# Output product of an attention layer from rounded parts, and a value product without its wholly masked blocks

## The reference

```python
x = x + attn(layernorm(x))            # x: 4 batches x 512 rows x 256
x = x + moe(layernorm(x))             # 8 experts, 2 per row, capacity 640, hidden width 1024

# attn: 32 query heads in 8 groups of 4 that share a key head and a value head; head width 64
q, k, v = split(x @ W_qkv); q, k = rope(q), rope(k)
mask = (q_pos >= k_pos) & (q_pos < k_pos + 64)
attn = where(mask, -inf, q @ k.T / 8)              # 512 x 512 for each head
w = softmax(concat(attn, sink))[..., :-1]
out = (w @ v) @ W_out                              # W_out: (32 * 64) x 256
```

## Time and profile before

| | |
|---|---|
| median of 3 runs | 1071.03 us (1070.24 to 1071.81) |
| span of the profiled execution, first to last instruction | 1063.8 us |
| period of a group inside the attention part, one example | 23.54 us |
| PE busy | 97% |
| DVE busy | 86% |
| ACT, POOL busy | 61%, 62% |

### The profile page before, as it was taken

How to read it: one execution, slowest core, us unless ns; L and a number is a source line. 1 busy time by engine, 2 the same in 40 slices (tenths; PEclk the granted TensorE clock), 3 DMA queues, 4 the chain that set the end, 5 groups by cost and what they waited for, 6 DMA issues and landing times.

```text
span 1063.8 us, 32339 instructions
## 1 busy us (share of the span) xinstructions
PE 1032.3 (97%) x13013; PEld 729.8 (69%) x13013; DVE 918.9 (86%) x1962; ACT 653.7 (61%) x1670; POOL 663.4 (62%) x607
## 2 busy tenths in 40 slices
PE   6899999999999999999999999999998999999996
PEld 4466666666666666666666666666566999999995
DVE  6999999999999999999999999999966777677773
ACT  4676667666667666667776656777654455544451
POOL 5657776767666888666777877667762422233332
PEclk8999999999999999999999999999999999999998
DMA  3544555544333344333343344333324344454421
GB/s 94 150 114 117 129 135 130 137 118 131 95 84 81 95 110 105 97 100 79 80 111 101 95 131 111 94 86 98 100 80 159 87 121 121 126 125 124 101 44 21
DMA packets 115574, 112.11 MB, mean 105 GB/s; under 512 B 35264, under 2 KB 103936, under 8 KB 115296
## 3 DMA queue, kind: packets, MB, share of 16 engines
q1 hardware_dynamic: 97648, 90.29, 31.3%
q0 software_dynamic: 7296, 8.55, 5.0%
q10 hardware_dynamic: 10480, 11.20, 3.8%
HBM read 74.84 MB, written 21.83 MB: 91 GB/s over the span
## 4 chain that ended last, share of the span: by engine, by line
PE 60%; DVE 35%; issue 2%; ACT 1%; DMA 0%; SPq 0%; POOLq 0%; DVEq 0%
PE bank L1536 21%; DVE probs_ring L1124 15%; DVE probs_t L1133 13%; PE bank L1701 11%; PE bank L1512 11%; PE bank L1712 7%; DVE heads_sb L1153 4%; PE bank L1715 4%; PE bank L1568 1%; PE bank L1441 1%; PE bank L1676 1%; PE bank L1458 1%; PE bank L1476 1%; PE bank L1596 1%; DVE neg_max L1124 0%
## 5 line engine op out<-in xcount | busy, mean ns | idle before, releaser
L841 ACT ACTIVATE probs_ring<-probs_ring,neg_max 128x512 f32<-128x512 f32 x512 | 365.9, 717 | 210.2 <-DVE neg_max L1124 209.4
L1124 DVE CUSTOM_DVE_ANT_0 probs_ring<-bank,mask,sink_neg 128x512 f32<-128x512 f32 x512 | 360.3, 738 | 24.9 <-PE bank L1512 23.8
L1133 DVE STREAM_TRANSPOSE probs_t<-probs_ring 128x1024 f32<-128x1024 f32 x256 | 317.8, 1241 | 0.2 <-ACT probs_ring L841 0.2
L1512 PE MATMUL bank<-qk_st 64*128 64x512 f32 x1024 | 280.6, 624 | 11.6 <-DVE neg_max L1124 7.4
L1536 PE MATMUL bank<-probs_t,v_quads 32*64 32x256 f32 x8192 | 247.9, 381 | 0.0
L1536 PEld LDWEIGHTS bank<-probs_t,v_quads 32*64 32x64 f32 x8192 | 179.3, 132 | 75.4 <-issue 48.1
L670 POOL TENSOR_TENSOR chunk_sb<-chunk_sb,rope_sb 128x512 f32<-128x512 f32 (+1 forms) x94 | 119.8, 1275 | 111.1 <-issue 80.6
L789 POOL DMA_INDIRECT out<-expert_sb,slots x40 | 77.8, 1945 | 150.6 <-DVE expert_sb L1385 143.3
L1512 PEld LDWEIGHTS bank<-qk_st 64*128 64x128 f32 x1024 | 85.3, 185 | 77.0 <-DVE neg_max L1124 41.5
L1043 ACT ACTIVATE hidden<-bank,b_sb 128x320 f32<-128x320 f32 x128 | 60.5, 524 | 107.1 <-PE bank L1701 107.1
L675 POOL TENSOR_TENSOR qk_st<-chunk_sb,swap_sb 128x512 f32<-128x512 f32 (+1 forms) x94 | 120.0, 1276 | 7.4
(11 more groups left out here) (189 smaller groups left out, 1352.5 us busy)
## 6 DMA issues: line engine op xcount, KB each, us to landing
v_quads<-v_rows SPq DMA_DIRECT2D x128, 128.0 KB
recip_wide<-recip_rows SPq DMA_DIRECT2D x64, 256.0 KB
w_raw<-in_L_ffn_w SPq DMA_DIRECT2D x14, 1024.0 KB, 8.2
swap_sb<-chunk_sb SPq DMA_DIRECT2D x314, 32.0 KB
w_raw<-in_L_attn_W_qkv SPq DMA_DIRECT2D x32, 256.0 KB, 2.9
slots<-slot_rows SPq DMA_DIRECT2D x9, 662.5 KB, 4.0
slot_rows<-x2T ACTq DMA_DIRECT2D x8, 662.5 KB, 6.2
w_raw<-in_L_attn_W_qkv SPq DMA_DIRECT2D x64, 64.0 KB, 2.7
```

The lines of the kernel that those rows point to most:

```text
L841: nc.scalar.activation(probs[(g * UNITS + n) % RING][:, :], probs[(g * UNITS + n) % RING][:, :], ACT.Exp, bias=neg_max[j][:, n:n + 1], sca ...
L1124: nc.vector.tensor_tensor_reduce(probs[(g * UNITS + n) % RING][:, :], SCORE[SCORE_OF[n // 2][n % 2]][:, :], mask[:, L - P - t * P:2 * L - ...
L1133: nc.vector.transpose(probs_t[j][:, :, (h // 2) * (2 * P):(h // 2 + 1) * (2 * P)] .rearrange("p b (h q) -> p h b q", h=2)[:, :, :, t * BLK ...
L1512: nc.tensor.matmul(SCORE[SCORE_OF[n // 2][hh]][:, :], qk_st[j][half, h // 2, t * P:(t + 1) * P], qk_st[j][half, PAIRS, :], start=True, sto ...
```

## The change

The output product of all groups but the last becomes three products of rounded parts, on the whole array. ACT rounds `heads_sb` to `heads_hi` (two instructions a group), POOL subtracts to get `heads_lo` (two), and PE does 24 matmuls of 128 rows x 256 columns in place of 16 of 64 rows. The weights are split once for each of the 8 key heads (ACT `wo_high`, POOL `wo_low`, in the first batch), stored to memory (`keep_wo`), and read back for each group of the later batches (`load_wo_again`). `recip_wide` now shares its memory with `heads_lo`, so the spreading of the reciprocals waits for the output product of the group before. The steps move: the halves of the output product to 30 and 32, the copies to 31 and 33, the residual to 35, and the sum of the rotation of Q01 from -11 to -9. The value product leaves out the 32 x 32 blocks that the band hides: such a matmul covers 3 of 4 blocks of rows, and where the hidden one is an inner block, the matmul becomes two.

```diff
-        Y_AT = {28: 0, 30: 1}
-        Y_FIRST_OUT_AT, Y_OUT_AT, RESIDUAL_AT = 30, 31, 38
+        HEADS_HI_AT, HEADS_LO_AT = {26: 0, 27: 1}, {22: 0, 24: 1}
+        WO_HI_AT, WO_LO_AT = 18, 19
+        Y_AT, LAST_Y_AT = {30: 0, 32: 1}, {28: 0, 30: 1}
+        Y_FIRST_OUT_AT, Y_OUT_AT, RESIDUAL_AT = 31, 33, 35
+        ROT_SUM_AT = {2: Q23, -12: KV, -9: Q01}
...
+        recip_wide = heads_lo[:, :, :].bitcast(F32)
...
             def recip_spread(g):
                 sp.wait_ge(s_recip_out, g * 16 + 16)
                 if later(2 * g):
-                    sp.wait_ge(s_heads, 2 * g + 1)
+                    sp.wait_ge(s_y, 2 * g + 1)
...
+            def keep_wo(k):
+                sp.wait_ge(s_wo_lo, k + 1)
+                sp.dma_start(wo_store[k], wo_parts[k % 2]...).then_inc(s_wo_kept, 16)
+            def load_wo_again(g):
+                sp.wait_ge(s_wo_kept, (g - 1) * 16 if g < NKV + 2 else NKV * 16)
+                sp.wait_ge(s_y, 2 * (g - 2) + 2 + 1)
+                sp.dma_start(wo_parts[g % 2]..., wo_store[g % NKV]).then_inc(s_wo_back[g % 2], 16)
...
+            def heads_low(g, half):
+                pool.wait_ge(s_heads_hi, 2 * g + half + 1)
+                nc.gpsimd.tensor_tensor(heads_lo[:, banks_of, :], heads_sb[:, banks_of, :],
+                                        heads_hi[:, banks_of, :].bitcast(F32), ALU.subtract).then_inc(s_heads_lo, 1)
...
+            def heads_high(g, half):
+                act.wait_ge(s_heads, 2 * g + half + 1 + 1)
+                nc.scalar.activation(heads_hi[:, banks_of, :], heads_sb[:, banks_of, :], ACT.Copy).then_inc(s_heads_hi, 1)
...
                     nc.scalar.activation(y_sb[1][:, 1, :], PV[3][:, 0:D], ACT.Copy).then_inc(s_y_first_out, 1)
+                    nc.scalar.activation(y_sb[1][:, 0, :], PV[1][:, 0:D], ACT.Copy).then_inc(s_y_out, 1)
...
-                    for a in range(QUADS):
+                    for i, a in enumerate((0, 1, 2, 3) if g == GROUPS - 1 else (1, 3, 0, 2)):
...
+            PV_ORDER = [(c, turn) for c in (0, 1, 2, 3) for turn in (1, 0, 2, 3)]
+            def value_step(j, c, turn, first, last):
+                for a in range(QUADS):
+                    d = (a + turn) % QUADS
+                    rows = slice(a * BLK, (a + 1) * BLK)
+                    hidden_tile = TPB * d + c + 1 - TPB * a
+                    tiles = [t for t in range(TPB) if t != hidden_tile]
+                    runs = [tiles[:hidden_tile], tiles[hidden_tile:]] if 0 < hidden_tile < TPB - 1 else [tiles]
+                    for p in range(PAIRS):
+                        ...
+                        for run in runs:
+                            q = slice(run[0] * BLK, (run[-1] + 1) * BLK)
+                            ins = nc.tensor.matmul(out[:, :, q], v_quads[j][rows, d, c * HD:(c + 1) * HD], seen[:, :, q],
+                                                   start=first, stop=last)
...
+                    for a in (3 - half, 1 - half):
+                        for h in range(2):
+                            for i, (heads, wo) in enumerate([(heads_hi, wo_hi), (heads_hi, wo_lo), (heads_lo, wo_hi)]):
+                                ins = nc.tensor.matmul(PV[a][:, 0:D], heads[:, a, h * P:(h + 1) * P], wo[:, h, :],
+                                                       start=(h == 0 and i == 0), stop=(h == 1 and i == 2))
+                        ins.then_inc((s_y_high, s_y)[half], 1)
```

More of the change, by code:

```diff
@@ L557, in _ @@
                 swap_halves(g + 1, Q23)
+                if 0 < g <= NKV:
+                    keep_wo(g - 1)
+                if g >= NKV:
+                    load_wo_again(g)
                 if g % NKV == 1 and g > NKV:
@@ L676, in rotate, with wo_low @@
                                         ALU.add).then_inc(s_rot, 1)
+            def heads_low(g, half):
+                pool.wait_ge(s_heads_hi, 2 * g + half + 1)
+                banks_of = odd_or_even(half)
+                nc.gpsimd.tensor_tensor(heads_lo[:, banks_of, :], heads_sb[:, banks_of, :],
+                                        heads_hi[:, banks_of, :].bitcast(F32), ALU.subtract).then_inc(s_heads_lo, 1)
+            def wo_low(k):
+                pool.wait_ge(s_wo_hi, k + 1)
+                hi, lo = [wo_parts[k % 2][:, part, :, :] for part in range(2)]
+                nc.gpsimd.tensor_tensor(lo, wo_raw[k % 2][:, :, :], hi.bitcast(F32), ALU.subtract).then_inc(s_wo_lo, 1)
             pool.wait_ge(s_small_in, 16)
@@ L680, in pool_step @@
                 if n in ROT_AT and (g > 0 or ROT_AT[n] == Q23):
-                    c = ROT_AT[n]
-                    rotate(g, j, c)
+                    rotate_products(g, ROT_AT[n])
+                if n in ROT_SUM_AT and (g > 0 or ROT_SUM_AT[n] == Q23):
+                    rotate_sum(g, j, ROT_SUM_AT[n])
+                if n in HEADS_LO_AT and g < GROUPS - 1:
+                    heads_low(g, HEADS_LO_AT[n])
+                if n == WO_LO_AT and g < NKV:
+                    wo_low(g)
                 if n == (SECOND_SPLIT_AT if g == 1 else SPLIT_AT) and 0 < g < GROUPS - 1:
@@ L838, in act_step @@
                     v_copy(g)
+                if n in HEADS_HI_AT and g < GROUPS - 1:
+                    heads_high(g, HEADS_HI_AT[n])
+                if n == WO_HI_AT and g < NKV:
+                    wo_high(g)
                 if 0 <= n < UNITS:
@@ L1530, in pe_step @@
                             pe.wait_ge(s_chunk_out, (g + 2) * CHUNKS + KV + 1)
-                    for blk in PV_AT[n]:
-                        c, d = divmod(blk, TPB)
-                        for a in range(QUADS):
-                            rows = slice(a * BLK, (a + 1) * BLK)
-                            for p in range(PAIRS):
-                                ins = nc.tensor.matmul(PV[a][p * HD:(p + 1) * HD, 0:2 * P],
-                                                       v_quads[j][rows, d, c * HD:(c + 1) * HD],
-                                                       probs_t[j][rows, blk, p * 2 * P:(p + 1) * 2 * P],
-                                                       start=(blk == 0), stop=(blk == BLOCKS - 1))
-                    if blk == BLOCKS - 1:
+                    for i in PV_AT[n]:
+                        ins = value_step(j, *PV_ORDER[i], first=(i == 0), last=(i == BLOCKS - 1))
+                    if i == BLOCKS - 1:
                         ins.then_inc(s_pv, 1)
@@ new lines, in pe_step @@
+                    pe.wait_ge(s_heads_lo, 2 * g + half + 1)
+                    if half == 0:
+                        if g < NKV:
+                            pe.wait_ge(s_wo_lo, g + 1)
+                        else:
+                            pe.wait_ge(s_wo_back[j], ((g - NKV) // 2 + 1) * 16)
+                    wo_hi, wo_lo = [wo_parts[j][:, part, :, :] for part in range(2)]
+                    for a in (3 - half, 1 - half):
[4 more added lines that the diff above has]
+                        ins.then_inc((s_y_high, s_y)[half], 1)
@@ new lines, in pe_step @@
+                if n in LAST_Y_AT and g == GROUPS - 1:
+                    half = LAST_Y_AT[n]
+                    pe.wait_ge(s_heads, 2 * g + half + 1 + 1)
+                    for a in (2 * half, 2 * half + 1):
+                        for h in range(2):
+                            ins = nc.tensor.matmul(
+                                PV[half][:, (a % 2) * D:(a % 2 + 1) * D], heads_sb[:, a, h * P:(h + 1) * P],
+                                wo_raw[j][:, h, :], start=(h == 0), stop=(h == 1))
+                    ins.then_inc(s_y, 1)
```

75 lines of the change are left out of this document (39 added, 36 removed).

## The result

The changed kernel takes 1187.88 us (median of 4 runs, 1185.96 to 1192.59) against 1071.42 us (4 runs, 1070.24 to 1071.86) for the kernel before on the same chip: a ratio of 1.1098, 95% interval 1.1072 to 1.1124. The direction is the one predicted. The size is not: 1123 us was forecast, and 1187.88 lies outside the range of 1090 to 1176.

The account below looks back on a forecast made before the run. A chain alternating between DVE and PE was taken as the bound, not PE alone. Per period 1.83 + 0.15 - 0.2 = 1.78 us, times 29 = 52, giving span 1116 and time 1123 us; range 1090 to 1176.

Parts of the forecast that it names:

- It applies in periods 2 to 30: Summing step: where a pair, an output half and scores 2 meet, 1.78 us a period, 29 x 1.78 = 52.
- scores 4 later: PE's queue: scores 4 stand behind pair 0, half 1, scores 2 and pair 1, starting at 14.3 instead of 12.47, +1.83 us.
- The order of scores, halves and pairs: PE's queue each period: scores 12, scores 14, half 0, scores 0, pair 0, half 1, scores 2, pair 1, scores 4.
- With the semaphore I take +0.15: Value product behind scores 4 waits for the output copies, now behind the chunk's copy on ACT: 15.5 against 15.4, +0.15 us.
- I go near the lower end: -0.2: Value product itself, bounds -0.35 (columns left out) and +0.6 net (additional matmuls): taken as -0.2 us.
- the serial rival: Value product's split matmuls run one behind the other: +2.2 us a group, 70 more, about 1190; chance 0.06.
- Cover is 0.8 us; what POOL is later than that adds one for one: POOL's heads_lo: first ends at 4.8, before half 0 at 5.6; second at 7.4, before the sink's argument at 7.71.
- So it has the room: POOL's residual and wo_low fit before the KV rotation, which waits for a chunk copy itself 1.8 later: no cost.
- The clock rival: PE's idle stretches drop its clock to the lower level: 29 x 1.75 = 51 us more, 1174; chance 0.12.
- its sign: What would show the lower PE clock: a granted clock under 0.95 in the attention part.
- the forecast added 7.2: Last step of the sum: the runs' median stands 7.2 us above the span, so span 1116 gives 1123.
- the expected saving of the three products: Output product on PE: a half takes 1.65 us in place of 1.73, so each saves only 0.08.

Follow-up runs that it names:

- Run 9: Changed kernel with ACT's last two copies of the output one unit earlier, ahead of the chunk's copy: 1172.09 us, ratio 1.0933.
- Run 6: Kernel before with value matmuls shortened only where the hidden block is at an edge, none cut in two: 1063.87 us, ratio 0.9947.
- run 1: Kernel before with only the change's value product, hidden blocks left out and two of sixteen steps with split matmuls: 1078.56 us, ratio 1.0116.
- run 5: Changed kernel with the route's scatters on POOL issued six units later, past the sink's sum: 1182.11 us, ratio 1.105.
- Run 8: Run 7's kernel with no value matmul cut (only edge blocks left out) and the last scatters ahead of the last group's heads_lo: 1102.03 us, ratio 1.0303.
- run 7: Changed kernel with output halves and copies in their old slots and the heads' parts made earlier on ACT and POOL: 1109.08 us, ratio 1.0373.
- Run 10: Changed kernel with one of the three output products (coarse parts only), all parts still made: 1173.5 us, ratio 1.0974.
- run 12: Run 8's kernel with one of the three output products, the two small ones left out: 1111.05 us, ratio 1.0388.
- run 4: Changed kernel with both output halves and the output copies back in their old slots: 1136.98 us, ratio 1.0681.
- run 3: Changed kernel with the first copies of the output one unit earlier on ACT, ahead of the last exponential and the sink's: 1149.65 us, ratio 1.0796.

## Why the prediction was right in direction and wrong in size

Scores 4 came late by the mechanism that was forecast. What failed are the sizes of the terms of one period, the value product's with its sign, and the step "It applies in periods 2 to 30", which let one period without route work stand for all and put the route's ten periods and the last two at nothing more. I take the terms of the sum in the group that starts at 699.33, 26.55 us, against the same group of the kernel before, 23.56 (not the one of the earlier trace rows, whose successor holds route work in the changed kernel). Starts are those of each piece's first record.

| term | predicted | measured |
|---|---|---|
| scores 4 later | +1.83 | +2.17 (12.49 to 14.66) |
| value product waits for copies | +0.15 | +0.58 (1.06 to 1.64) |
| value product itself | -0.2 | +0.24 |
| sum a period | +1.78 | +2.99 (the quiet ones: +3.12 on average) |
| POOL behind the halves | 0 | 11.1 us in all, in seven periods |
| DVE beside POOL | 0 | 5.8 us in all, in three periods |
| the rest of the route's ten periods | 0 | 2.8 us in all |
| last two periods | 0 | +6.8 us |

**The order of scores, halves and pairs held, and nearly to the tenth.** Scores 14 at 4.62 (predicted 4.6), half 0 at 5.67 (5.6), scores 0 at 7.29 (7.2), pair 0 at 9.11 (9.0). The idle stretches are 1.05 by DVE and 0.69 by ACT's copy, and DVE waits 1.76 before unit 2. A half takes 711.65 - 710.03 = 1.62 (1.65). Of the 0.34 that are missing 0.1 is there when pair 0 starts, and the rest comes after: pair 0 took 1.59, priced at 1.40; scores 2 and pair 1 took 2.35, priced at 2.25. The 1.40 was read from a place where no full-array work followed, and now a half follows; that this is the reason was not tried. The mechanism was right, its size short.

**"With the semaphore I take +0.15" failed.** I added the chunk's copy and the two `y` copies up to 15.5 and set it against 15.4, but left out that the chunk's copy starts 0.23 after scores 4 do, and that the value matmul follows the copies by another 0.26. The wait was there, priced at a quarter of its size. Run 9 shows the whole term: taken away, it gives 0.65 a quiet period.

**"I go near the lower end: -0.2" failed in sign.** The lower bound was the columns saved, the upper one the cuts. Run 6 and run 1 split them: -0.18 and +0.40 a group. Each was inside its bound (-0.35 and +0.93). The choice between them was made with no row for it, and it was the wrong one. The rule by which the serial rival was priced, from the Trainium skill ("TensorE: Matmul & The Clock Gate", part 3, the mechanism), would have made the cuts cost 2.2. Run 1 does not bear that out; its cuts cost 0.40 a group.

**"Cover is 0.8 us; what POOL is later than that adds one for one" named the right path and was not followed up.** It prices POOL from one period, and the 0.8 is half 0's cover. The scatters stand behind the second `heads_lo`, and there the prediction's own times leave 7.71 - 7.4 = 0.3 (measured 0.48). Seven periods have two scatters in just that place: the sink's argument is 1.95 late, and PE idles 2.2 to 2.5 us before pair 0 in place of 0.69: 31.0 - 29 x 0.69 = 11 us. In three of the seven, those that end at groups 14, 22 and 29, the clock also fell, within 1.3 us of the end of that wait. The seven exceed the quiet 3.12 by 13.9 in all; the 2.8 beyond the waits lie in these three. Moving the scatters gave 10.2 back in the ten periods, and there the clock fell in none of them (run 5).

**"So it has the room" counted POOL's room and not DVE's beside it.** The other three periods, those that end at groups 12, 20 and 28, exceed 3.12 by 5.8 us in all (6.1 in run 5, with the scatters moved). In them DVE has small instructions of the route late in the period. In the kernel before they ran in POOL's idle time ahead of the KV rotation. Now DVE comes to them 2.5 to 4.2 us later, and the rotation starts at most 0.4 later, so the two run side by side. Changed kernel, DVE, then POOL, and the third of the DVE lines in the kernel before:

```profile
605.65 0.21 DVE L1385 TENSOR_REDUCE slot_f<-picked 128x8 f32<-128x64 f32 x1
605.90 0.43 DVE L1388 TENSOR_TENSOR full<-slot_f,slot_end 128x8 f32<-128x8 f32 x1
606.36 1.19 DVE L1389 SCALAR_TENSOR_TENSOR scatter_idx<-full,slot_f 128x8 uint32<-128x8 f32 x1
607.94 1.05 DVE L414 TENSOR_TENSOR xn<-gates,top_sum 128x32 f32<-128x32 f32 x1
```
```profile
605.03 1.27 POOL L702 TENSOR_TENSOR chunk_sb<-chunk_sb,rope_sb 64x512 f32<-64x512 f32 x1 [1.76 <-issue]
606.27 1.26 POOL L703 TENSOR_TENSOR swap_sb<-swap_sb,rope_sb 64x512 f32<-64x512 f32 x1
607.60 1.26 POOL L713 TENSOR_TENSOR qk_st<-chunk_sb,swap_sb 64x512 f32<-64x512 f32 x1
```
```profile
535.43 0.17 DVE L1315 SCALAR_TENSOR_TENSOR scatter_idx<-full,slot_f 128x8 uint32<-128x8 f32 x1
```

The last three DVE instructions end 0.03, 0.02 and 0.13 us after POOL's L702, L703 and L713. In the whole attention part nine DVE instructions are lengthened like this, from 0.16 to 0.19 us each to between 0.30 and 2.64, by 8.6 us together: 4.4, 2.1 and 2.0 in just these three periods. In the kernel before none is. No run moved them by themselves, so that they are the periods' excess is read from the trace and not tried.

**The last two periods were not looked at.** The last scatters feed a chain (scatter, gather, turning on PE) that the last value product waits for, and both `heads_lo` of group 30 came ahead of them. Run 8, with the scatters in front, has 19.69 where run 7 has 25.79.

**The clock was not the cause, nor innocent.** Inside the attention part the clock fell five times against once before. At 1.75 each the four additional falls are at most 7 of the 117 us. The clock rival (one in each period) is refuted: the granted clock is 0.988, and its sign was one under 0.95. In runs 10 and 12, where PE has less to do between its waits, the clock spends more time at the lower level (48 us against 17, and 27 against 7).

**Does it add up?** 29 x 3.12 = 90.5, scatters 11.1, DVE beside POOL 5.8, the rest of the ten periods 2.8, the last two periods 6.8: 117.0. The forecast had 51.6 of it. What it lacked is 29 x (3.12 - 1.78) = 38.9 in terms that it had and sized too small, 19.7 in the route's ten periods and 6.8 in the last two, both put at nothing. From there to the runs' medians the forecast added 7.2; the median stands 3.9 above the new span.

**Where the expected saving of the three products went.** Run 10 answers it from the other end. Even with two thirds of them gone the kernel is 1.0974. The length of the output product is paid once a period, in half 1's place; what costs is that its operands need a step on ACT and one on POOL between `heads_sb` and PE. In late slots (the changed kernel) that pushes scores 2; in early ones (runs 4, 7, 8) PE waits for POOL. Of the 0.110, the slot of one copy gives 0.030, all slots back 0.042, and earlier parts 0.031 more. (The first and the second overlap: run 4 moves the copy too. The runs were made in different batches, and each figure is a difference of two ratios, good to about 0.005.) After run 8, 0.030 stay. In it POOL has no gap between the parts and PE still waits 0.34; the rest of its 0.69 a period I did not divide further, so it stays open.

## What to carry to other kernels

Before an operation is split into parts for PE's sake, count what must happen between its operand and PE on the other engines, and place it in *every* kind of period, those with the route's transfers and the last ones too, since a cover of less than 1 us read in one period is gone in the next. When a step moves in time, look also at what runs beside it on the other engines, DVE beside POOL above all. When a step moves in a queue, check what now stands ahead of each copy that releases its bank: two numbers in the table of slots (runs 3 and 9) held 0.030 and 0.017 of the time. Leaving out hidden columns pays where the matmul just gets shorter, and costs where it must be cut in two.

## What the runs showed of the hardware

- The value product has 16 steps of eight matmuls on eight tiles, four row groups by two column groups. Two of these steps with one block of four left out at an edge (of all eight matmuls in one, of six in the other) gain 0.18 us a group; two steps of which each matmul is cut in two cost 0.40 a group against leaving them whole. The tiles still run side by side after a cut: 96 records, 32 of them short, take 2.59 us where 80 whole ones take 2.41.

```profile
374.35 2.59 PE L1587 MATMUL bank<-probs_t,v_quads 32*64 32x256 f32 x96 [0.60 <-DVE probs_t L1207]
```
```profile
625.62 2.41 PE L1536 MATMUL bank<-probs_t,v_quads 32*64 32x256 f32 x80
```

(The first is the changed kernel, the second the kernel before, both the first of a group's three segments.)

- Less work on PE made a kernel slower: run 12 against run 8, 1.0388 against 1.0303, with the granted clock at 0.981 against 0.990. In the stretch shown PE had waited 2.07 us for POOL right before the clock fell to its lower level.

- Short DVE instructions that read two operands in the on-chip buffer (`TENSOR_TENSOR`, `SCALAR_TENSOR_TENSOR`) lasted until just after the end of a POOL `TENSOR_TENSOR` that ran beside them: nine of them took 0.30 to 2.64 us in place of 0.16 to 0.19. A `TENSOR_REDUCE` with one operand beside the same POOL work kept its 0.21. Of the 27 such two-operand instructions in each trace's attention part none lies inside a POOL instruction.
